# Two root chains of a tile joined and moved to GpSimd, and one ScalarE step issued a quarter later

## The reference

```
x = x + 0.5 * ffn(layernorm(x))
gate_up = einsum('bsh,oh->bso', x, w_gu); gate, up = gate_up[..., :I], gate_up[..., I:]
h = silu(gate) * up
y = einsum('bsi,hi->bsh', h, w_down)
ffn = y / sqrt(mean(y * y) + 1e-6)
```

## Time and profile before

| | |
|---|---|
| time, median of 3 runs | 2605.78 us (2604.2 to 2606.3) |
| the profiled execution | 2607.0 us, its span 2605.0 us |
| granted TensorE clock, mean | 0.995 |
| busy: PE, DVE, ACT, POOL | 2490.2, 1858.1, 1466.6, 1495.7 us |
| chain that ended last, by line | PE pp L97 10%, PE ps L97 4%, POOL sb L106 2%, ACT sb L103 1%, DVE sb L112 1% |
| DMA | 130.58 MB, mean 50 GB/s |

### The profile page before, as it was taken

One profiled execution on the slowest core, in us unless ns is written; L12 is line 12 of the kernel. 1 busy time (PEld: TensorE's weight loads), 2 busy tenths in 40 slices (PEclk: granted clock), 3 DMA queues, 4 the chain that ended last, 5 costly groups with the idle time before them and its releaser, 6 DMA issues. The chain is left out here.

```text
span 2605.0 us, 39715 instructions
## 1 busy us (share of the span) xinstructions
PE 2490.2 (96%) x14559; PEld 1088.2 (42%) x14559; DVE 1858.1 (71%) x3352; ACT 1466.6 (56%) x2829; POOL 1495.7 (57%) x1357
## 2 busy tenths in 40 slices
PE   6899999999999999999999999999999999999998
PEld 3444444444443344433344434434333444444443
DVE  7877777768759594948586695858566777777765
ACT  6666666665225656566622256565664566666664
POOL 3466666664325767676442266676774466666665
PEclk9999999999999999999999999999999999999999
DMA  2012211121122020200230312020005201111101
GB/s 66 17 47 70 96 41 49 49 98 49 49 59 60 6 51 6 67 6 3 72 141 33 80 41 53 6 67 6 3 4 194 74 25 41 49 49 49 49 33 49
DMA packets 78017, 130.58 MB, mean 50 GB/s; under 512 B 19551, under 2 KB 24698, under 8 KB 77694
## 3 DMA queue, kind: packets, MB, share of 16 engines
q1 hardware_dynamic: 77822, 128.05, 15.9%
HBM read 68.23 MB, written 31.46 MB: 38 GB/s over the span
## 5 line engine op out<-in xcount | busy, mean ns | idle before, releaser
L106 POOL TENSOR_TENSOR sb<-sb,sb 128x512 f32<-128x512 f32 (+6 forms) x1341 | 1488.1, 1135 | 1093.6 <-ACT sb L103 428.0
L97 PE MATMUL pp<-sb,sb 128*128 128x512 f16 (+8 forms) x11230 | 2071.5, 420 | 40.9 <-DVE sb L112 14.0
L97 PEld LDWEIGHTS pp<-sb,sb 128*128 128x128 f16 (+3 forms) x11230 | 795.9, 102 | 1082.6 <-issue 212.4
L97 PE MATMUL ps<-sb,sb 128*128 128x512 f16 (+8 forms) x2786 | 725.7, 349 | 43.2 <-ACT sb L103 17.1
L103 ACT ACTIVATE sb<-pp 128x512 f32<-128x512 f32 (+6 forms) x1035 | 521.3, 561 | 316.4 <-PE pp L97 308.2
L103 ACT ACTIVATE sb<-sb 128x512 f16<-128x512 f32 (+4 forms) x513 | 329.0, 649 | 455.1 <-DVE sb L112 335.2
L118 DVE TENSOR_REDUCE sb<-pp 128x1 f32<-128x512 f32 (+3 forms) x704 | 441.3, 668 | 148.7 <-PE pp L97 148.4
L112 DVE SCALAR_TENSOR_TENSOR sb<-ps,sb,sb 128x512 f32<-128x512 f32 x437 | 318.4, 747 | 137.1 <-PE ps L97 77.3
L97 PEld LDWEIGHTS ps<-sb,sb 128*128 128x128 f16 (+3 forms) x2786 | 241.6, 98 | 374.4 <-DVE sb L112 68.5
L112 DVE SCALAR_TENSOR_TENSOR sb<-pp,sb,sb 128x512 f32<-128x512 f32 x447 | 324.1, 745 | 84.1 <-PE pp L97 82.6
L103 ACT ACTIVATE sb<-ps 128x512 f32<-128x512 f32 (+5 forms) x473 | 263.4, 568 | 148.7 <-PE ps L97 123.9
(11 more groups left out here) (27 smaller groups left out, 364.0 us busy)
## 6 DMA issues: line engine op xcount, KB each, us to landing
sb<-sb SPq DMA_DIRECT2D x144, 128.0 KB, 2.4
sb<-L_attn_X SPq DMA_DIRECT2D x64, 256.0 KB, 3.4
sb<-xa SPq DMA_DIRECT2D x64, 256.0 KB, 4.2
sb<-xc SPq DMA_DIRECT2D x64, 256.0 KB, 3.4
xa<-sb SPq DMA_DIRECT2D x32, 256.0 KB, 2.0
xc<-sb SPq DMA_DIRECT2D x32, 256.0 KB, 4.3
out<-sb SPq DMA_DIRECT2D x32, 256.0 KB, 2.0
sb<-sb SPq DMA_DIRECT2D x48, 96.0 KB, 2.1
```

Of the source, the lines that this page charges most:

```text
L97: return self.e.matmul(*a, **k) if self.e else self
L106: return self.e.tensor_tensor(*a, **k) if self.e else self
```

## The change

First, both chains of a tile are computed together: eight columns, four for the next tile's layernorm and four for the last tile's rms, in `w8` (three 128x8 rows) and `rr` (the results, `rs` and `r4` side by side). This is done in tiles 1 to 6 of both stages. Four steps stand on VectorE (`roots_dve`: two scaled inputs at (4,0), shift and guess at (4,1)), and then 15 instructions on GpSimd (`roots_pool`), in 13 steps at (4,2), (4,3), (5,0), (5,1) and (5,2). The first four of the 17 `roots` entries are only VectorE's. Tile 0 keeps `isd` and tile 7 keeps `rms` on VectorE, where they were. ScalarE's first application to the next tile moves from (5,2) to (5,3), the last from (6,3) stays.

Second, `h1` is issued at quarter 1 of the next block and no more at quarter 0, in all tiles.

Third, the two weight pieces of a block in stage 1 share one semaphore, and TensorE waits for both.

```diff
         self.ones = take([128, 32], F32, 128)
         self.st = take([128, 4, 6], F32, 96)
         self.mv = take([128, 4, 2], F32, 32)
-        self.rs = take([128, 4], F32, 32)
+        self.rr = take([128, 8], F32, 32)
+        self.rs, self.r4 = self.rr[:, 0:4], self.rr[:, 4:8]
+        self.w8 = take([128, 3, 8], F32, 96)
         self.w4 = take([128, 3, 4], F32, 48)
         self.ss = take([128, 4], F32, 32)
-        self.r4 = take([128, 4], F32, 32)
         self.w5 = take([128, 3, 4], F32, 48)
         self.bias = take([128, 4, 4], F32, 64)
         self.bvb = take([128, 512], F32, 2048)
...
         self.added, self.silu_done, self.h_made = (p.sign(n + x) for x in ("added", "silu_done", "h_made"))
         self.h1_made, self.h2_made, self.down_done = (p.sign(n + x) for x in ("h1_made", "h2_made", "down_done"))
         self.y_copied, self.squared, self.x_out = (p.sign(n + x) for x in ("y_copied", "squared", "x_out"))
+        self.rms_root, self.isd_root = p.sign(n + "rms_root"), p.sign(n + "isd_root")
+        self.guessed, self.rooted = p.sign(n + "guessed"), p.sign(n + "rooted")
         self.isd_made, self.rms_made, self.y_scaled = (p.sign(n + x) for x in ("isd_made", "rms_made", "y_scaled"))
         self.last_h, self.last_h2 = p.sign(n + "last_h"), p.sign(n + "last_h2")
         self.final_out = p.sign(n + "final_out")
...
                         yield "group", tt, i, c, u
                     for u in (1, 0) if c == 0 else (0, 1):
                         yield "evac", tt, i, c, u
-                    if c == 0 and n:
+                    if c == 1 and n:
                         yield "h1", n - 1
                     if c == 1 and n:
                         yield "h2", n - 1
...
             first = self.deq and tt == 0
             steps = self.norm_v(tt + 1)
             place(steps[:4], v(6, 7) if first else v(1, 2), (1, 1, 1, 1))
-            place(steps[4:], v(8, 9) if first else v(3, 4), (4, 2, 4, 3))
-            place(self.norm_a(tt + 1), a(9, 9) if first else a(5, 6), (2, 2) if first else (1, 1, 1, 1))
+            if tt:
+                place([("roots", tt)] * 17, ((4, 0), (4, 1), (4, 2), (4, 3), (5, 0), (5, 1), (5, 2)), (2, 2, 3, 3, 3, 2, 2))
+            else:
+                place(steps[4:], v(8, 9) if first else v(3, 4), (4, 2, 4, 3))
+            place(self.norm_a(tt + 1), a(9, 9) if first else ((5, 3), (6, 1), (6, 2), (6, 3)), (2, 2) if first else (1, 1, 1, 1))
         elif self.ph == 0:
             place([("ahead_norm",)] * 24, v(3, 4, 7, 8, 9, 10), (2,) * 12)
         if tt:
             place(self.finish_a(tt - 1), a(2, 3), (1, 1, 1, 1))
-            place(self.finish_v(tt - 1), v(5, 6), (4, 2, 4, 2))
+            if tt + 1 == NT:
+                place(self.finish_v(tt - 1), v(5, 6), (4, 2, 4, 2))
             place(self.finish_y(tt - 1), a(7, 8), (1, 1, 1, 1))
         return out
...
         elif what == "apply":
             tt, tb = at
             x = p.xb[tb][:, :]
-            e.wait_ge(*f.isd_made.at(tt))
+            e.wait_ge(*(f.isd_root if tt > 1 else f.isd_made).at(tt))
             e.activation(x, x, ACT.Identity, scale=p.rs[:, tb:tb + 1], bias=p.w4[:, 0, tb:tb + 1]).then_inc(
                 *f.normed.up((tt, tb)))
         elif what == "last" and at[0] < NT - 1:
             tt, tb = at
             y = p.ysb[tb][:, :]
-            e.wait_ge(*f.rms_made.at(tt))
+            e.wait_ge(*(f.rms_root if tt < NT - 2 else f.rms_made).at(tt))
             e.activation(y, y, ACT.Copy, scale=p.r4[:, tb:tb + 1]).then_inc(*f.y_scaled.up((tt, tb)))
         elif what == "square" and not f.final(at[0]):
             tt, tb = at
...
             if ("n", tt) not in gens:
                 gens["n", tt] = isd_dve(e, p, f, tt)
             next(gens["n", tt])
+        elif what == "roots":
+            tt = at[0]
+            if ("q", tt) not in gens:
+                gens["q", tt] = roots_dve(e, p, f, tt)
+            next(gens["q", tt], 0)
         elif what == "decode":
             i, k = at
             if ("d", i) not in gens:
...
     yield from rsqrt_dve(e, p, p.rs[:, :], p.mv[:, :, 1], 1.0, 1e-5, 1.0, p.w4)
     e.wait_ge(*p.V.now())
     e.scalar_tensor_tensor(p.w4[:, 0, :], p.mv[:, :, 0], -1.0, p.rs[:, :], ALU.mult, ALU.mult).then_inc(*f.isd_made.up(tt))
+    yield
+
+
+def roots_dve(e, p, f, tt):
+
+    V = p.V
+    v, g, t = p.w8[:, 0, :], p.w8[:, 1, :], p.w8[:, 2, :]
+    e.wait_ge(*V.now())
+    e.tensor_scalar(v[:, 0:4], p.mv[:, :, 1], 1.0, 1e-5, ALU.mult, ALU.add).then_inc(*V.up())
+    yield
+    e.wait_ge(*f.squared.at((tt - 1, 3)))
+    e.tensor_scalar(v[:, 4:8], p.ss[:, :], 4.0 / D, 4e-6, ALU.mult, ALU.add).then_inc(*V.up())
+    yield
+    e.wait_ge(*V.now())
+    e.tensor_scalar(t.bitcast(I32), v.bitcast(I32), 1, None, ALU.logical_shift_right).then_inc(*V.up())
+    yield
+    e.wait_ge(*V.now())
+    e.tensor_scalar(g.bitcast(I32), t.bitcast(I32), -1.0, float(0x5F3759DF), ALU.mult, ALU.add).then_inc(
+        *f.guessed.up(tt))
+    yield
+
+
+def roots_pool(e, p, f, tt):
+
+    R = f.rooted
+    v, g, t = p.w8[:, 0, :], p.w8[:, 1, :], p.w8[:, 2, :]
+    e.wait_ge(*f.guessed.at(tt))
+    e.tensor_scalar(v, v, -0.5, None, ALU.mult).then_inc(*R.up())
+    e.tensor_tensor(t, g, g, ALU.mult).then_inc(*R.up())
+    for n in range(3):
+        e.wait_ge(*R.now())
+        e.tensor_tensor(t, t, v, ALU.mult).then_inc(*R.up())
+        yield
+        e.wait_ge(*R.now())
+        e.tensor_scalar(t, t, 1.5, None, ALU.add).then_inc(*R.up())
+        yield
+        e.wait_ge(*R.now())
+        e.tensor_tensor(p.rr[:, :] if n == 2 else g, t, g, ALU.mult).then_inc(
+            *(f.rms_root.up(tt - 1) if n == 2 else R.up()))
+        if n < 2:
+            yield
+            e.wait_ge(*R.now())
+            e.tensor_tensor(t, g, g, ALU.mult).then_inc(*R.up())
+        yield
+    e.wait_ge(*f.rms_root.at(tt - 1))
+    e.tensor_scalar(t[:, 0:4], p.mv[:, :, 0], -1.0, None, ALU.mult).then_inc(*R.up())
+    yield
+    e.wait_ge(*R.now())
+    e.tensor_tensor(p.w4[:, 0, :], t[:, 0:4], p.rs[:, :], ALU.mult).then_inc(*f.isd_root.up(tt + 1))
     yield
...
 def ffn_pool(e, p, f, plan):
+    roots = {}
     for what, *at in plan:
         if what in ("scaled", "weight"):
             todo = [at[0]] if what == "scaled" else [at[0] + 2] if at[0] + 2 < 3 * IC else []
...
                     e.wait_ge(*f.h_made.at(n - 1))
                 e.tensor_tensor(p.h[n % 2][:, :], p.sil[n % 2][:, :], p.acc[1][n % 3][:, :], ALU.mult).then_inc(
                     *f.h_made.up(n))
+        elif what == "roots":
+            tt = at[0]
+            if tt not in roots:
+                roots[tt] = [4, roots_pool(e, p, f, tt)]
+            roots[tt][0] -= 1
+            if roots[tt][0] < 0:
+                next(roots[tt][1])
         elif what == "last" and at[0] < NT - 1:
             tt, tb = at
             x = p.xr[tb][:, :]
...
             if f.deq:
                 e.wait_ge(*f.w_kept.at(3 * i + u))
             else:
-                e.wait_ge(*f.wg_in[i].at(0))
+                e.wait_ge(*f.w_in[i].at(1))
             w = p.wg[:, IC - 1 - i, c, u, :]
             e.matmul(bank, w, p.x1[tt % 2][:, c, :], start=True, stop=False)
             e.matmul(bank, w, p.x2[tt % 2][:, c, :], start=False, stop=True).then_inc(*f.gu_done.up((tt, i, c, u)))
```

More of the change, by code:

```diff
@@ L312, in __init__ @@
         else:
-            self.wg_in, self.wd_in = ([p.sign(f"{n}{x}_in{i}", 16) for i in range(IC)] for x in ("wg", "wd"))
+            self.w_in = [p.sign(f"{n}w_in{i}", 16) for i in range(IC)]
         self.plan = list(self.order())
@@ L527, in ffn_pe @@
             else:
-                e.wait_ge(*f.wd_in[i].at(0))
+                e.wait_ge(*f.w_in[i].at(1))
             e.matmul(y, h1[:, c], p.wd[:, i, 0, :], start=i == 0, stop=False)
@@ L1899, in load_piece_sp @@
     s, d = weight_pieces(p, i)[u]
-    e.dma_start(s, d).then_inc(*(f.wg_in, f.wd_in)[u][i].up(0))
+    e.dma_start(s, d).then_inc(*f.w_in[i].up(u))
 def tensor_program(e, p):
```

## The result

| | before | after |
|---|---|---|
| median of 4 runs each, us | 2604.99 (2604.01 to 2606.30) | 2581.20 (2580.69 to 2581.73) |
| span of the profiled execution, us | 2605.0 | 2579.8 |
| clock, mean | 0.995 | 0.995 |
| middle tile, us | 70.89 | 68.90 |

The ratio is 0.9907, interval 0.9892 to 0.9922: 23.8 us faster. The forecast was 2586 with a range of 2569 to 2604.

A forecast was written before the change was run, and what follows sets the result against it. TensorE, busy 96%, bounds the kernel; only its stalls can be saved. 31.2 - 8.8 + 2.0 + 0 - 1.4 - 3.6 = 19.4 us off 2607.0 gives 2587.6, median 1.2 lower: forecast 2586, range 2569 to 2604.

The forecast's parts named there:

- Middle tiles: Tiles 1 to 6 of each stage: 31.2 us saved from lost TensorE time, less 8.8 for a new stall.
- the collision: VectorE's shift and guess in block 4 meet GpSimd's earlier add: a new 0.73 us stall per middle tile, 8.8 in all.
- The three stalls and the slips: TensorE's losses per middle tile: 0.53 us ending block 2, 0.90 each in blocks 8 and 9, slips 0.29; all to go.
- The chain on GpSimd: Small steps moved to GpSimd, 0.25 us each, stay hidden in blocks 4 to 6: cost 0, range 0 to 38 us.
- The last tile: Tile 7 of stage 1: 3.4 us of stalls and slips go, two collisions cost 0.75 each; gain 2.
- stalls 2 and 3: TensorE's stalls in blocks 8 and 9, 0.90 us each, waiting for a bank behind the high half; to go.
- Tile 7 of stage 0: Also carries attention's first norm on VectorE: five collisions cost 3.6 us against 3.4 saved, counted as nothing.
- Tile 0 of stage 1: Collisions at (3,1) and (4,1) lose about 0.75 + 0.95 us for 0.3 saved: -1.4.
- The unpacking tile: Tile 0 of stage 0: four unpacking instructions collide instead of two, costing VectorE 0.45 us in 8 blocks, -3.6.
- A: Rival: VectorE's collisions with GpSimd do not happen or cost nothing, gain 31 + 3 or so, 2571 us; chance 0.18.
- B: Rival: GpSimd's chain is dear, from about 0.42 us per step eating the gain; at 0.5, 2625 us; chance 0.13.
- C: Rival: TensorE's stalls only change place, 20 of the 31 us come back, 2606 with collisions; chance 0.09.

The follow-up runs named there:

- experiment 3: The changed kernel with VectorE's shift and guess at (4,0) in place of (4,1): 2571.64 us against 2606.68 for the kernel before, ratio 0.9864.
- experiment 1: The kernel before with only the high half issued at quarter 1 of the next block, both chains still on VectorE: 2612.50 us against 2606.68, ratio 1.0023.
- Experiment 5: The changed kernel with a spare 128x4 instruction ahead of 13 steps of GpSimd's chain: 2621.85 us against 2606.12 for the kernel before, ratio 1.0061.
- experiment 2: The changed kernel with the high half back at quarter 0, the joined chain still on GpSimd: 2635.28 us against 2606.68 for the kernel before, ratio 1.0109.
- experiment 7: The kernel of experiment 6 with the high half back at quarter 0 in tile 0 of stage 0: 2564.80 us against 2606.12 before, ratio 0.9844.
- experiment 6: The kernel of experiment 3 with VectorE's small chain work in tiles 0 and 7 moved to quarter 0: 2565.41 us against 2606.12 before, ratio 0.9845.

## Why the prediction was right, and where a size was off

In spans after is 25.2 us shorter; the prediction's sum was 19.4.

- **Middle tiles.** Forecast 12 x 2.6 = 31.2 less 8.8 for the collision, 22.4, or 1.87 a tile. Measured 1.99 a tile, 23.9. The three stalls and the slips are gone; the new stall is 0.65 for a forecast 0.73, since the pair ended 0.07 sooner than I counted. That both numbers are what they seem was shown from both sides: the stall goes with the collision (experiment 3), and it comes, four times over, with the high half alone (experiment 1).
- **The chain on GpSimd.** Forecast 0. No stall in block 5 or 6, at 0.28 a step for 0.25. The margin named as 0.2 us in block 6 was spent: ScalarE's application was at 6.85 of block 5 (forecast 6.6), and VectorE's evacuation of (2, up) in block 6 at 5.25 for a deadline of 5.24. That the term came out at 0 with nothing to spare is in part luck: the chain ends at 6.81 of block 5 for a forecast 6.5. Experiment 5 shows the price beyond it.
- **The last tile.** Forecast +2.0. The stretch from tile 6's first turn to the end went from 109.92 to 105.63; 1.8 of the 4.29 are stalls 2 and 3 of tile 6, which lie in it, so 2.5 for the tile.
- **Tile 7 of stage 0.** Forecast five collisions, 3.6 for 3.4, nothing. Measured five stalls, 3.85. The stretch gained 1.25 with the same 1.8 in it, so the tile lost 0.55.
- **Tile 0 of stage 1.** Forecast -1.4. Both stalls are there (0.64 and 1.01 for 0.75 and 0.95), yet the stretch from attention's end to the first turns lost only 0.47: at the tile's start two waits of TensorE, 0.94 for ScalarE and 1.09 for VectorE as the brackets of before have them, became one of 1.36. That is the high half's doing: with it alone (experiment 1) there is the one wait of 1.36 and a stretch of 47.05, with the chains alone (experiment 2) the two, 0.95 and 1.09, and 46.60. The prediction had no term for the tile's start.
- **The unpacking tile: the term that was mis-sized.** Forecast -3.6 (0.45 in 8 blocks), measured at most about -1 (experiment 7). The step that failed is "four unpacking instructions collide instead of two". It read two from the earlier trace rows; in the timeline of VectorE before, the next row there is a third, 0.82 for an instruction that takes 0.34 to 0.35 when free:

```profile
59.03 1.46 DVE L109 TENSOR_SCALAR sb<-sb 128x384 uint16<-128x384 uint16 x2
60.41 0.82 DVE L106 TENSOR_TENSOR sb<-sb,sb 128x384 uint16<-128x384 uint16 x1
```

and in that of after, at the same place:

```profile
59.04 2.71 DVE L109 TENSOR_SCALAR sb<-sb 128x384 uint16<-128x384 uint16 x4 [0.20 <-POOL sb L106]
61.67 0.34 DVE L106 TENSOR_TENSOR sb<-sb,sb 128x384 uint16<-128x384 uint16 x1
```

Counted one by one in the traces of the whole tile, 26 of the 132 unpacking instructions take over 0.4 us before and 28 after; two more in each of 8 blocks would have been 16 more. In the groups of the first 130 us, before, the two forms read:

```profile
L109 DVE TENSOR_SCALAR sb<-sb 128x384 uint16<-128x384 uint16 x88 | 28.6, 366 | 2.8 <-POOL sb L106 1.2 <-DMA sb<-L_ffn_down_packed 0.5
...
L106 DVE TENSOR_TENSOR sb<-sb,sb 128x384 uint16<-128x384 uint16 x44 | 16.9, 405 | 0.0
```

and after:

```profile
L109 DVE TENSOR_SCALAR sb<-sb 128x384 uint16<-128x384 uint16 x88 | 30.6, 388 | 2.5 <-POOL sb L106 1.1 <-DMA sb<-L_ffn_down_packed 0.2
...
L106 DVE TENSOR_TENSOR sb<-sb,sb 128x384 uint16<-128x384 uint16 x44 | 14.9, 359 | 0.0
```

One form pays 2.0 more and the other 2.0 less; the sum is 45.5 both times. GpSimd's work moved against VectorE's, and hit other instructions instead of more of them.

Of the 5.8 us by which the spans beat the sum, this term makes 2.6 to 3.6, the one above 0.9, the middle tiles 1.5 and the last tile 0.5; tile 7 of stage 0 gave 0.55 less than forecast. Nearly all errors go one way, so the hit is not one of errors that cancel. Two of the prediction's small sums don't come out as written and change nothing: 16 transposes at 0.11 are 1.76 and not 1.74, and eight steps of 0.25 from 5.47 end at 7.5 and not 7.2.

The rivals: A (collisions cost nothing) fell with the 2.08 us pair, though its time of 2571 is what experiment 3 reached by taking the collision away. B's condition was not met. C (stalls only change place) fell: TensorE waits nowhere in blocks 7 to 10 of a middle tile.

## What to carry to other kernels

Before a wait is taken out of a chain, list what runs on the other engines at the time to which its successor moves: here a GpSimd instruction came one microsecond earlier and blocked small VectorE work that had been harmless. Two edits that each cost time (+6 and +29 us) gave -24 together, so measure the combination and not the parts alone. Small work goes where the partner is idle or where a long evacuation is not yet due: moving the first guess by one quarter was worth some 8 of the 9.1 us by which that kernel's span is shorter. Where the partner has no pause, as in block 8 of experiment 6, an earlier quarter helps less.

## What the hardware did that I had not expected

On GpSimd the one-input TENSOR_SCALAR on 128x8 takes 237 ns and the two-input TENSOR_TENSOR 203. At this size a second input did not make the instruction dearer.

What a small VectorE instruction loses is set by GpSimd's instruction and not by its own size: two of 128x4, 0.35 us alone, took 2.07 beside two GpSimd instructions in a row (experiment 1), and the integer pair on 128x8 took 2.08.
